# Stacks of queries and keys by four transfers in place of seven, with fixed bias rows and a fourth slot

## The reference

```python
for i in range(4):
    q, k, v = heads(x @ Wi.T + bi)                 # 16 heads, dim 8
    scores = einsum('bhqd,bhkd->bhqk', q, k) / sqrt(8)
    scores = scores + slope[h] * (pos_k - pos_q) + causal
    x = layer_norm(x + (softmax(scores) @ v) @ Wo.T + bo)
    x = layer_norm(x + gelu(x @ W1.T + b1) @ W2.T + b2)
```

## Time and profile before

| | us |
|---|---|
| median of 3 runs | 3035.25 (3028.97 to 3037.77) |
| the profiled execution | 3035.09 |
| its span, first to last instruction | 3033.3 |
| PE busy (matmuls) | 2454.7, 81% |
| DVE busy | 1850.0, 61% |
| ScalarE (ACT) busy | 1391.1, 46% |
| GpSimd (POOL) busy | 548.0, 18% |
| mean granted clock of PE | 0.87 |

### The profile page before, as it was taken

How to read it: one execution, slowest core, us unless ns; L and a number is a source line. 1 busy time by engine, 2 the same in 40 slices (tenths; PEclk the granted TensorE clock), 3 DMA queues, 4 the chain that set the end, 5 groups by cost and what they waited for, 6 DMA issues and landing times. The chain is left out here.

```text
span 3033.3 us, 38272 instructions
## 1 busy us (share of the span) xinstructions
PE 2454.7 (81%) x12564; PEld 1014.7 (33%) x12564; DVE 1850.0 (61%) x4413; ACT 1391.1 (46%) x2373; POOL 548.0 (18%) x636
## 2 busy tenths in 40 slices
PE   5779989999998999998668798794556796988738
PEld 3323333333433433333233323341122342323215
DVE  3656766666676766777235675447999324867242
ACT  2345556565666556565425223335332431556420
POOL 1200111010111111010007300004796001100000
PEclk7778999999998999999868899887899795999768
DMA  2111112121122212111010000002343011112020
GB/s 92 73 61 53 65 63 74 62 74 58 60 77 77 70 54 76 59 68 51 19 34 1 21 1 25 0 9 94 117 146 112 5 39 66 64 73 70 23 84 14
DMA packets 76777, 173.15 MB, mean 57 GB/s; under 512 B 21990, under 2 KB 37606, under 8 KB 72494
## 3 DMA queue, kind: packets, MB, share of 16 engines
q1 hardware_dynamic: 76580, 170.70, 16.1%
HBM read 129.93 MB, written 39.71 MB: 56 GB/s over the span
## 5 line engine op out<-in xcount | busy, mean ns | idle before, releaser
L1062 ACT ACTIVATE sb_prob<-ps 128x512 f32<-128x512 f32 (+1 forms) x1520 | 810.3, 575 | 591.5 <-PE ps L852 382.3
L826 PE MATMUL ps<-sb_k_stack_half,sb_q_stack_half 78*128 78x512 bf16 (+3 forms) x1920 | 608.0, 351 | 116.5 <-DMA sb_q_stack_half<-alibi 43.2
L852 PE MATMUL ps<-sb_q_stack_half,sb_k_stack_half 81*128 81x128 bf16 (+2 forms) x2240 | 589.6, 321 | 65.7 <-ACT sb_prob L1062 54.2
L963 DVE TENSOR_REDUCE sb_row_max<-ps 128x1 f32<-128x512 f32 x640 | 433.7, 688 | 217.7 <-PE ps L826 216.0
L972 DVE CUSTOM_DVE_ANT_0 sb_masked_scores<-ps,sb_mask_row 128x128 bf16<-128x128 f32 (+3 forms) x640 | 284.4, 488 | 199.1 <-PE ps L826 198.3
L972 DVE CUSTOM_DVE_ANT_0 sb_masked_scores<-ps,sb_mask_row,sb_row_max 128x128 bf16<-128x128 f32 (+3 forms) x640 | 342.1, 544 | 101.7 <-PE ps L826 98.1
L852 PEld LDWEIGHTS ps<-sb_q_stack_half,sb_k_stack_half 81*128 81x128 bf16 x2240 | 205.0, 100 | 413.3 <-ACT sb_prob L1062 189.0
L873 PE MATMUL ps<-sb_prob,sb_v_first_half 128*9 128x512 f32 (+3 forms) x2560 | 315.4, 567 | 0.2 <-ACT sb_o_raw L1069 0.2
L826 PEld LDWEIGHTS ps<-sb_k_stack_half,sb_q_stack_half 78*128 78x128 bf16 x1920 | 189.3, 103 | 341.1 <-DVE sb_row_max L972 86.6
L2253 PE MATMUL ps<-sb_read_out,sb_ident 128*128 128x512 f32 x256 | 138.5, 673 | 121.3 <-DVE sb_read_out L2340 115.4
L2307 POOL TENSOR_TENSOR sb_inflow<-sb_delta_u,sb_b_spread 128x1024 f32<-128x1024 f32 x64 | 201.4, 3161 | 27.1 <-DVE sb_states L2329 19.0
(11 more groups left out here) (360 smaller groups left out, 3281.9 us busy)
## 6 DMA issues: line engine op xcount, KB each, us to landing
sb_q_stack_half<-q_rows SPq DMA_DIRECT2D x240, 96.0 KB
sb_k_stack_half<-k_rows SPq DMA_DIRECT2D x120, 192.0 KB
o_rows<-sb_o_raw SPq DMA_DIRECT2D x80, 256.0 KB, 4.1
sb_b_spread<-b_rows SPq DMA_DIRECT2D x32, 512.0 KB, 4.8
sb_c_spread<-c_rows SPq DMA_DIRECT2D x32, 512.0 KB, 3.7
sb_k_stack_half<-k_rows SPq DMA_DIRECT2D x120, 96.0 KB
q_rows<-sb_qk_parts SPq DMA_DIRECT2D x60, 128.0 KB, 2.6
k_rows<-sb_qk_parts SPq DMA_DIRECT2D x60, 128.0 KB, 2.1
```

What stands on the lines that cost most here:

```text
L826: pe.matmul(M.ps[:, k % RING, 0:hi - lo], qst[half][0:S1_ROWS, s, j, at:at + P], kst[half][0:S1_ROWS, s, lo // CH, j, 0:hi - lo], start=Tr ...
L852: mm = pe.matmul(bank[:, x * w + lo:x * w + hi], kst[half][0:S2_ROWS, s, t // 4, j, t % 4 * P:(t % 4 + 1) * P], qst[half][0:S2_ROWS, s, j, ...
L963: dve.reduce_max(rowmax[:, tau % 3, 0, at:at + 1], M.ps[:, k % RING, 0:w], AX_X).then_inc(first_done, 1)
L1062: act.activation(prob[:, st % PROB_STEPS, heads[0]:heads[-1] + 1, a:CH], scores.rearrange("p (j q) -> p j q", j=len(heads)), ACT.Exp).then ...
```

## The change

A stack is four transfers: one for the keys, in which every one of the 24 (part, dimension) rows is repeated three times, and three for the queries, dimension first and part second. The DRAM tensors are laid out by part, dimension, group of heads, so that 24 rows lie at one step; the order of the weights' columns and of the rotation tables follows. The bias rows are loaded once, at the start, into every slot; for that a slot must always hold the same group of heads, so the transformer has four slots for the second half too, and slot number is group number. In the last attention the second half keeps three slots, since its bias rows are all the same. PE waits for 64 per use of a slot in place of 112.

```diff
-HALF_SLOTS = (4, 3)
...
-            self.slot.append(seen[half] % HALF_SLOTS[half])
-            self.use.append(seen[half] // HALF_SLOTS[half])
+            self.slot.append(seen[half] % slots[half])
+            self.use.append(seen[half] // slots[half])
...
-                        sp.dma_start(out[part, :, :, b, c].rearrange("g d j t -> (g d) j t"),
+                        sp.dma_start(out[part, :, :, b, c].rearrange("d g j t -> (d g) j t"),
                                      parts[:, u % 2, part, :]).then_inc(parts_out[u % 2], 16)
...
-                    q_rows = D["q_rows"][l % 2, :, g, :, b, half].rearrange("s d j t -> s d (j t)")
-                    k_rows = D["k_rows"][l % 2, :, g, :, b].rearrange("s d c j t -> s d (c j t)")
+                    q_rows = D["q_rows"][l % 2, :, :, g, b, half].rearrange("s d j t -> s d (j t)")
+                    k_rows = D["k_rows"][l % 2, :, :, g, b].rearrange("s d c j t -> s d (c j t)")
                     width = GROUP * CH * (half + 1)
+                    sp.dma_start(kst[half][0:PAIR_ROWS, s].rearrange("r c j t -> r (c j t)"),
+                                 k_rows[:, :, 0:width].rearrange("p d w -> (p d) w").unsqueeze(1)
+                                 .to_broadcast([3 * DH, 3, width])).then_inc(sem, 16)
                     for part in range(3):
                         at = 3 * DH * part
-                        sp.dma_start(kst[half][at:at + 3 * DH, s].rearrange("r c j t -> r (c j t)"),
-                                     k_rows[part, :, 0:width].unsqueeze(0).to_broadcast([3, DH, width])).then_inc(sem, 16)
-                        sp.dma_start(qst[half][at:at + 3 * DH, s].rearrange("r j t -> r (j t)"), q_rows).then_inc(sem, 16)
-                    sp.dma_start(qst[half][PAIR_ROWS:S1_ROWS, s].rearrange("r j t -> r (j t)"), F.alibi[g]).then_inc(sem, 16)
+                        sp.dma_start(qst[half][at:at + 3 * DH, s].rearrange("r j t -> r (j t)"),
+                                     q_rows.rearrange("p d w -> d p w")).then_inc(sem, 16)
...
                 for h in range(2):
-                    for s in range(HALF_SLOTS[h]):
+                    for s in range(SLOTS[h]):
                         sp.dma_start(kst[h][PAIR_ROWS:S2_ROWS, s].rearrange("r c j t -> r (c j t)"),
                                      aux[:, 0:GROUP * CH * (h + 1)]).then_inc(aux_in, 16)
-                sp.wait_ge(aux_in, 16 * sum(HALF_SLOTS))
+                        sp.dma_start(qst[h][PAIR_ROWS:S1_ROWS, s].rearrange("r j t -> r (j t)"),
+                                     F.bias_rows[s]).then_inc(aux_in, 16)
+                sp.wait_ge(aux_in, 32 * sum(SLOTS))
...
-                        pe.wait_ge(stack_in[half][s], 16 * 7 * (plan.use[tau] + 1))
+                        pe.wait_ge(stack_in[half][s], 64 * (plan.use[tau] + 1))
...
-        decoder(nc, M, D, Form(LAYERS, True, False, [D["alibi"][g * 6:g * 6 + 6] for g in range(NGRP)], col,
+        decoder(nc, M, D, Form(LAYERS, True, False, (NGRP, NGRP), [D["alibi"][g * 6:g * 6 + 6] for g in range(NGRP)], col,
...
-        decoder(nc, M, D, Form(1, False, True, [D["no_bias"]] * NGRP, col, lambda l: 16 * len(loads),
+        decoder(nc, M, D, Form(1, False, True, (NGRP, 3), [D["no_bias"]] * NGRP, col, lambda l: 16 * len(loads),
...
-            D = {**D, name: nc.dram_tensor(name, (2, 3, NGRP, DH, B, 2, GROUP, CH), BF16, kind="Internal").ap()}
+            D = {**D, name: nc.dram_tensor(name, (2, 3, DH, NGRP, B, 2, GROUP, CH), BF16, kind="Internal").ap()}
...
-    rows = np.tile(np.repeat(np.arange(DH), GROUP), NGRP)
+    rows = np.repeat(np.arange(DH), NGRP * GROUP)
...
-    perm = np.arange(P).reshape(NGRP, GROUP, DH).transpose(0, 2, 1).reshape(P)
+    perm = np.arange(P).reshape(NGRP, GROUP, DH).transpose(2, 0, 1).reshape(P)
```

More of the change, by code:

```diff
@@ L356, with __init__ @@
     S1_NS, DVE_FIX, PV_SWITCH = 0.42, 70, 200
-    def __init__(self, layers, ffn, rotate):
+    def __init__(self, layers, ffn, rotate, slots):
         self.layers, self.ffn, self.rotate = layers, ffn, rotate
@@ L635, with __init__ @@
 class Form:
-    def __init__(self, layers, ffn, rotate, alibi, col, weights_at, affine, gain=None, tables=None, loads=()):
-        self.layers, self.ffn, self.rotate, self.alibi, self.col = layers, ffn, rotate, alibi, col
+    def __init__(self, layers, ffn, rotate, slots, bias_rows, col, weights_at, affine, gain=None, tables=None, loads=()):
+        self.layers, self.ffn, self.rotate, self.col = layers, ffn, rotate, col
+        self.slots, self.bias_rows = slots, bias_rows
         self.weights_at, self.affine, self.gain, self.tables, self.loads = weights_at, affine, gain, tables, loads
 def decoder(nc, M, D, F, W=None):
-    plan = Plan(F.layers, F.ffn, F.rotate)
+    SLOTS = F.slots
+    plan = Plan(F.layers, F.ffn, F.rotate, SLOTS)
     col = F.col
@@ L656, in decoder @@
         vb = sb("v_second_half", [P, B, 4, HEADS, DH + 1])
-        qst = [sb(f"q_stack_half{h}", [S2_ROWS, HALF_SLOTS[h], GROUP, CH], BF16) for h in range(2)]
-        kst = [sb(f"k_stack_half{h}", [S2_ROWS, HALF_SLOTS[h], h + 1, GROUP, CH], BF16) for h in range(2)]
+        qst = [sb(f"q_stack_half{h}", [S2_ROWS, SLOTS[h], GROUP, CH], BF16) for h in range(2)]
+        kst = [sb(f"k_stack_half{h}", [S2_ROWS, SLOTS[h], h + 1, GROUP, CH], BF16) for h in range(2)]
         prob = sb("prob", [P, PROB_STEPS, GROUP, CH])
@@ L696, in place @@
             return a, CH - a, t >= 4 * half
-        names = ([f"stack{h}_in{s}" for h in range(2) for s in range(HALF_SLOTS[h])]
-                 + [f"rows{h}_in{s}" for h in range(2) for s in range(HALF_SLOTS[h])])
+        names = ([f"stack{h}_in{s}" for h in range(2) for s in range(SLOTS[h])]
+                 + [f"rows{h}_in{s}" for h in range(2) for s in range(SLOTS[h])])
         with phase(nc, *names, "cleared", "ones_set", "first_ready", "first_done", "max_split", "s2_ready", "unit_done",
@@ L704, in decoder @@
                    "parts_out0", "parts_out1", "weights_in", "aux_in", "rotated", "x_added") as (block, *sems):
[L705 to L708, removed]
+            n0 = SLOTS[0]
+            stack_in = (sems[:n0], sems[n0:n0 + SLOTS[1]])
+            sems = sems[sum(SLOTS):]
+            rows_in = (sems[:n0], sems[n0:n0 + SLOTS[1]])
             (cleared, ones_set, first_ready, first_done, max_split, s2_ready, unit_done, pv_done, o_saved, o_out0,
              o_out1, o_in0, o_in1, recip_ready, recip_out0, recip_out1, recip_in0, recip_in1, o_normed, side_ready, side_free, squared, rstd_ready, normed, gelu_done, hi_ready,
-             rest_ready, mid_ready, lo_ready, parts_out0, parts_out1, weights_in, aux_in, rotated, x_added) = sems[sum(HALF_SLOTS):]
+             rest_ready, mid_ready, lo_ready, parts_out0, parts_out1, weights_in, aux_in, rotated, x_added) = sems[sum(SLOTS):]
             o_out, o_in, parts_out = (o_out0, o_out1), (o_in0, o_in1), (parts_out0, parts_out1)
```

## The result

The changed kernel takes 2910.98 us (median of 4 runs, 2908.05 to 2936.34) against 3033.64 us before; the ratio is 0.9623, 95% interval 0.9566 to 0.968. Two later series of the same program gave 2908.00 us (ratio 0.9573, 0.952 to 0.9625) and 2908.58 us (0.9567, 0.954 to 0.9595).

A forecast was written before the change was run, and what follows sets the result against it. PE was taken to idle behind stack transfers carried by only three DMA engines. Idle time of 79 us plus 15 us of clock, less 4 for covered waits, took 3035 to 2945 us; range 2924 to 2990.

The forecast's parts named there:

- What bounds the kernel: Both decoders: PE idles because each stack's large transfers, outermost source dimension 3, run on three DMA engines at 76 GB/s.
- (a): Key and query transfers: outer dimensions 24 and 8 spread over more engines, 200 GB/s, 5.5 us from first issue to use.
- the ten other waits of the transformer: PE's waits for stacks in the transformer besides the first stack's: all go, 30 us.
- The two starts: First stack of each decoder: from first issue to use 11.1 us falls to 5.5, 11 us for both.
- (b): SP's issues: seven per stack become four, saving SP 2.0 us per stack, worth nothing by itself; key issue 0.75 us.
- (c): Bias rows loaded once per slot at each decoder's start: added issues fit into existing cover, worth nothing.
- (d): Fourth second-half slot, transformer only: alone about 20 us of stack waits, nearly nothing beside the faster transfers.
- The waits for maxima and sums: Transformer rows queued behind stacks: two PE waits for maxima go, 10 us; VectorE's waits for sums give 7 us.
- the clock: PE at 1.2 GHz after removed waits: 30 us lost in eleven stretches, half counted as regained, 15 us.
- A: Stack transfers: engines don't spread or bring no bandwidth, only the fourth slot counts; 3013 us, chance 0.07.
- B: PE's idle time: half returns as waits on ScalarE and VectorE, clock not regained; 2995 us, chance 0.08.
- C: Stack transit: more engines bring less bandwidth, 64 GB/s, lengthening waits; 24 us slower, 3059 us, chance 0.04.

The follow-up runs named there:

- the profile at 2936: Changed kernel, no further edit, against the kernel before: the execution profiled with the first result, at the slower level; 2936.34 us, series median 2910.98 us.
- the profile at 2914: Changed kernel run again unedited as the control, against the kernel before: its profiled execution took 2913.63 us; series median 2908.00 us, ratio 0.9573.

## Why the prediction was right or wrong

**What bounds the kernel** was read rightly: stack transfers on three engines, seen as PE idle. Outermost size 8 alone brings four fifths of the gain (101 of 126 us), and the changed kernel with size 3 loses 87 of them.

**(a)** The engines follow the outermost size. 200 GB/s were taken and 152 to 179 measured; 5.5 us from issue to use were taken and 7.2 and 8.6 measured, inside the bounds of 4.5 and 9. The term came out nonetheless: of the ten other waits of the transformer all went. The slot has a small part in that: with three slots one of 2.8 us is left. In the last attention 21 us were booked and 15.7 came (21.6 down to the 5.9 that the entry of 15.5 holds beside its 9.6); the two waits left there went with a fourth slot. The two starts: 11 us booked, 3.9 and 4.3 came (13.40 to 9.53, 13.87 to 9.6), about 8. By the rule of the Trainium skill, "DMA: Bandwidth & Descriptors", section "Why a DMA increments its semaphore by 16 and not by 1", the largest number up to 16 that divides both outermost sizes, keys run on 12 engines and queries on 8. The trace agrees: the share of 0.58, 9.3 engines, lies between the two, and with 8 for both it is 0.43, 6.9 engines, under SP's slower issues. The other rule of the Trainium skill that was weighed, in "SBUF — State Buffer", section "Door 1: The DMA port swizzle", gives six ports to 24 partitions, by an estimate at 27.2 GB/s each 163 GB/s for a query transfer. The measured 152 to 179 GB/s, of key and query transfers together, are of that size; no run here tells it from other causes.

**(b)** The key issue of 72 rows took 0.77 to 0.91 us where 0.75 were taken, 3.0 us for a stack. **(c)** was nothing, as said: 16 issues ran from 40.40 us and the first query parts went out at 61.80, as before at 61.59; in the last attention 14 ran from 2405.67 and the query parts went out at 2429.56. **(d)** The slot adds nearly nothing beside spread engines: 2.3 us of idle time. Alone, in the transformer, it was worth the 20 us booked.

**The waits for maxima and sums** went as booked. 10 us were booked for the maxima and 9.8 came (10.6 to 0.8). 7 us were booked for the sums; PE's waits on VectorE are down 6.5 us (14.6 to 8.1), and VectorE waits for no sums any more between 60 and 1400 us.

Idle time in all: 79 us forecast, 72.2 measured at the usual level and 70.6 at the slower one.

**The step that failed is the clock**, "eleven such stretches, 80.1 us in all ... I count half, 15 us", with 30 us as the most. In its place 51.3 us of busy time went at the usual level of the changed kernel and 29.3 at the slower one. The mechanism was right and the term was mis-sized: how much time at half clock would go. I counted 40 us of it. By the last column of the table the two decoders ran 467 us at half clock before, and 359 (the profile at 2936) or 313 (that at 2914) after: 108 or 154 us less. The price for each of these microseconds was if anything high: 29.3 / 108 and 51.3 / 154 are 0.27 and 0.33 us, where 0.38 was taken; PE stands idle in a part of them.

Two errors are in the count. I counted only the stretches behind the waits that go, and took those behind ScalarE's pauses as fixed, since the pauses stay. They do stay, and are 2.90 us in both profiles, but the stretch behind one is 10 us long in one and 3.4 in the other. From 410 us to the transformer's last feed-forward part the kernel before ran 139 us at half clock and the changed one 78 (the profile at 2914) or 112 (that at 2936), 61 or 27 us less, while only four of the eleven counted stretches, 14 us, lie there. And I halved the count for "waits on ScalarE that stay", which made the term smaller still. With 29 us in place of 15 the sum is 2931, in the range; with the 51 us of the usual level it is 2909, close to the measured 2911 and outside of any range that I drew.

Why the stretches behind unchanged pauses are shorter in most executions of the changed kernel is open: no run isolates it, and one program shows both lengths. Idle time removed does not by itself fix the clock's share. The fourth slot alone took 20.5 us of idle time in the transformer and 1.4 of busy time, the changed kernel with size 3 the same 20.1 and 17.6; but with one profile each, and busy times that differ by 23 us within one program, that is a hint and not a proof.

**The rivals.** A put the change at 3013 if only the slot counted. Its condition is false. The run that makes it true is the changed kernel with size 3, at 2995.3: the 20 us of idle time were right, and the 2 us of clock too low, with 25.0 us less busy time in the two decoders of its one profile. B: the 50 us of waits on ScalarE did not grow. C: more engines brought more bandwidth, 152 GB/s or more against 64 in the nine-row case. C's sum has a slip: a first-half stack without its bias rows, 590 kB at 64 GB/s against 614 at 76, takes 1.1 us more and not 1.6, so the two starts lose 2 us and not 3.

## What to carry to other kernels

When one stack of transfers is late, look at the DMA share while it is in transit before counting its bytes or its instructions: 0.19 of 16 engines names the cause, and a reordering of two source patterns, with no byte moved less, brought 101 of 126 us. Do not let a small broadcast or part index stand outermost by habit: 3 there held a transfer to three engines, 8 and 24 did not. More engines are not enough alone, as the nine-row transfer with its 64 GB/s shows. And on a kernel whose matrix engine is granted half its clock behind pauses, sum the time at half clock over the whole part that changes (467 us here) before pricing it, count the stretches behind the pauses that stay as well, and give the term both ends: here it was between 29 and 51 of the 100 to 124 us that the two decoders gained.

## What the runs showed of the hardware

The same pause of 2.90 us at the same place of the same program is followed by 3.4 us at 1.2 GHz in one execution and by 10 us in another, at five such places in each. Executions of the changed kernel lay at 2908 to 2911 us and at 2936 to 2939 in the first series and between 2899 and 2921 in the later ones, while the idle time of the transformer was 127.4, 126.0 and 125.3 us in the three profiles.

With outermost size 3 a single transfer of 72 rows moved no faster than three of 24: 77 GB/s. With 24 and 8 the share of engines tripled and the rate doubled, 76 to 81 against 152 to 179 GB/s: worked out from share and rate, an engine moves 25 to 27 GB/s with three of them at work and 16 to 19 with nine.
